# Cross-attention and routed FFN on one core: a transposition's copy on another engine, the router's scratch in another bank, and written-out orders for start and end

## What is computed

```python
def _L0_xattn_ref(input, encoded_features, Wq, bq, Wkv, bkv, Wo, bo):
    q = (input @ Wq + bq).reshape(b, tq, H, D).transpose(0, 2, 1, 3)
    kv = (encoded_features @ Wkv + bkv).reshape(b, tk, 2, H, D).transpose(2, 0, 3, 1, 4)
    scores = jnp.einsum('bhqd,bhkd->bhqk', q, k) / math.sqrt(D)
    attn = jax.nn.softmax(scores, axis=2)
    out = jnp.einsum('bhqk,bhkd->bhqd', attn, v)
    return out @ Wo + bo
def _L0_ffn_ref(x, w_router, w_block):
    scores = jnp.einsum('bld,d->bl', x, w_router)
    _, top_idx = jax.lax.top_k(scores, k)          # k = 96 of 128
    processed = jax.nn.gelu(jnp.einsum('bkd,de->bke', selected, w_block))
    return x.at[batch_idx, top_idx].set(processed)
x = x + _L0_xattn_ref(_layernorm(x), ctx, ...)
x = x + _L0_ffn_ref(_layernorm(x), w_router, w_block)
```

## Time and profile before

| what | value |
|---|---|
| runs | 956.96, 955.37, 956.26 us; median 956.26 |
| profiled execution, own time | 957.89 us |
| its span | 956.0 us |
| its mean granted TensorE clock | 0.985 |
| busy in the span | PE 892.5 (93%), ACT 894.6 (94%), DVE 849.6 (89%), POOL 814.4 (85%) |
| DMA | 70.84 MB, mean 74 GB/s |
| chain that ended last | PE 88%, ACT 5%, issue 2%, POOL 2% |

### The profile page before, as it was taken

The page is one execution under the profiler, slowest core; times in us unless marked ns, Lnnn a source line. Parts: engine busy times, 40 slices in busy tenths (PEclk is TensorE's granted clock), DMA queues, the critical chain, the costliest instruction groups (busy, mean ns, idle before and its releaser), DMA issues.

```text
span 956.0 us, 33133 instructions
## 1 busy us (share of the span) xinstructions
PE 892.5 (93%) x10276; PEld 757.0 (79%) x10276; DVE 849.6 (89%) x2568; ACT 894.6 (94%) x4612; POOL 814.4 (85%) x1514
## 2 busy tenths in 40 slices
PE   3699999999999999999999999999999999999870
PEld 2578888888888888888888888888888888888750
DVE  5688899999999999999999999999999999998754
ACT  2699999999999999999999999999999999999950
POOL 5257878999999999999999999999999999988777
PEclk9999999999999999999999999999999999999995
DMA  5222212322232232223223222322222232221102
GB/s 155 76 63 64 68 45 71 89 66 75 85 86 60 82 88 70 72 84 91 56 83 88 71 72 84 90 56 83 87 70 73 83 91 57 82 66 46 35 23 77
DMA packets 71245, 70.84 MB, mean 74 GB/s; under 512 B 12192, under 2 KB 62880, under 8 KB 71072
## 3 DMA queue, kind: packets, MB, share of 16 engines
q1 hardware_dynamic: 71072, 68.73, 25.2%
HBM read 35.13 MB, written 16.78 MB: 54 GB/s over the span
## 4 chain that ended last, share of the span: by engine, by line
PE 88%; ACT 5%; issue 2%; POOL 2%; DVE 1%; SPq 1%; DMA 1%; POOLq 0%; ACTq 0%; DVEq 0%
PE ps_q L272 18%; PE ps_s L306 14%; PE ps_a L355 13%; PE ps_a L279 12%; PE ps_t L279 11%; PE ps_a L272 9%; PE ps_t L327 8%; ACT e_sb L477 4%; PE ps_q L342 3%; DMA x_sb<-in_x 1%; POOL x_sb L834 1%; SPq L234 0%; POOL z_sb L817 0%; DVE neg_max L551 0%; PE ps_t L441 0%
## 5 line engine op out<-in xcount | busy, mean ns | idle before, releaser
L477 ACT ACTIVATE e_sb<-ps_s,neg_max 128x128 f32<-128x128 f32 x2048 | 724.9, 459 | 1.2 <-DVE neg_max L551 1.0
L477 ACT ACTIVATION_READ_ACCUMULATOR e_sb<-ps_s,neg_max 128x1 f32 x2048 | 588.3, 299 | 0.0
L551 DVE TENSOR_REDUCE neg_max<-ps_s 128x4 f32<-128x512 f32 x512 | 332.0, 669 | 64.4 <-PE ps_s L306 62.2
L306 PE MATMUL ps_s<-q_eo,k_sb 32*128 32x256 f32 x2048 | 146.8, 399 | 15.9 <-ACT e_sb L477 6.4
L768 POOL TENSOR_TENSOR v_pad<-v_sb,recip 128x256 f32<-128x256 f32 x128 | 79.6, 622 | 78.1 <-DVE recip L589 78.0
L355 PE MATMUL ps_a<-e_sb,v_pad 128*32 128x128 f32 x4096 | 138.4, 276 | 0.7 <-DVE x_sb L559 0.6
L279 PE MATMUL ps_a<-w_o_sb,o_sb 128*128 128x256 f32 x512 | 135.9, 388 | 2.9 <-DVE v_sb L635 2.4
L279 PE MATMUL ps_t<-w_z_sb,xt_sb 128*128 128x258 f32 x512 | 133.4, 383 | 2.9 <-DVE z_sb L646 2.9
L306 PEld LDWEIGHTS ps_s<-q_eo,k_sb 32*128 32x128 f32 x2048 | 95.8, 184 | 45.4 <-issue 42.4
L355 PEld LDWEIGHTS ps_a<-e_sb,v_pad 128*32 128x32 f32 x4096 | 104.1, 109 | 22.4 <-issue 21.2
L758 POOL TENSOR_TENSOR x_sb<-x_sb,bo_sb 128x256 f32<-128x256 f32 x128 | 121.3, 947 | 0.2
(11 more groups left out here) (80 smaller groups left out, 2249.2 us busy)
## 6 DMA issues: line engine op xcount, KB each, us to landing
x_sb<-in_x SPq DMA_DIRECT2D x64, 256.0 KB, 2.9
c_sb<-in_ctx SPq DMA_DIRECT2D x64, 256.0 KB, 3.1
q_eo<-q_raw SPq DMA_DIRECT2D x512, 32.0 KB, 2.0
out<-z_sb SPq DMA_DIRECT2D x64, 256.0 KB, 2.4
z_sb<-in_L_xattn_Wkv SPq DMA_DIRECT2D x2, 256.0 KB, 5.1
z_sb<-in_L_xattn_Wq SPq DMA_DIRECT2D x1, 256.0 KB, 2.9
w_o_sb<-in_L_xattn_Wo SPq DMA_DIRECT2D x1, 256.0 KB, 6.5
w_z_sb<-in_L_ffn_w_block SPq DMA_DIRECT2D x1, 256.0 KB, 5.5
```

The source lines that it names most:

```text
L306: mm = nc.tensor.matmul(ps_s[:, bank(b, j), c, :, :], k_sb[rows, r2, c, h * T:(h + 1) * T], q_eo[rows, r2, :, c, h, :], start=True, stop=True)
L477: last = nc.scalar.activation(e_sb[:, b % 4, j, c, par, :], ps_s[:, bank(b, j), c, par, :], ACT.Exp, bias=neg_max[:, b % 4, h:h + 1], accu ...
L551: nc.vector.tensor_reduce(neg_max[:, b % 4, :].rearrange("p (c j q) -> p j c q", c=C, j=J)[:, j, :, :], ps_s[:, bank(b, j), :, :, :], AX.X ...
```

## The change

It has five parts; names are those of the code.

1. `x1_transposed` (the copy of `ps_q`'s transposed x1 to xt_sb) goes from ACT to DVE, where it is the first work of each slot, ahead of the two aggregations and `maxima(s,3)`.
2. `fence` is gone: the aggregations and router steps carry their waits themselves.
3. The router's two transpositions write the fifth bank of `ps_s`. They wait for `exp_ready[0]` of an odd batch, `block_product` waits for the router no more, and in its place `scores(b)` waits for `cand_ready` when b mod 8 is 5 and for `keep_col_ready` when it is 1. The mean of the block weights goes through `ps_a`.
4. The first slots (up to the scores of batch 1) are written out for each engine. x of batches 2 and 3 is loaded fifth, not ninth; queries(0) stand behind the second transposition of inputs, not the third; batch 1's inputs are transposed into `ps_a`; the memset of q_eo is on POOL; the biases' semaphore is split; PE starts with 20 transpositions of the identity that nothing reads.
5. Behind the last scores each engine has an order of its own. `values(127)` goes ahead of `attention(126)`; the square in gelu of batches 123 to 127 is on ACT, the `(tanh+1)*z` of 121 to 127 is one instruction on DVE instead of two on POOL; `unprocessed` of 115 to 119 and 123 to 127 is on ACT; the router's last group runs in one piece.

The core of the diff (the order lists of the start and of DVE's and POOL's end are cut):

```diff
             return J if j == 0 and b % 2 == 1 else j
...
+        ps_cand, ps_keep, ps_mean = ps_fifth[0:GROUP, 0:T], ps_fifth[:, T:T + GROUP], ps_a[:, 0:ZW]
+        def inputs_bank(b):
+            return ps_a if b == 1 else ps_t
...
             load_c(0)
             sp.dma_start(raw_w["k"], w_kv[:, 0:E].rearrange("(c p) e -> p c e", p=P)).then_inc(w_in["k"], 16)
+            load_x(2)
...
-            load_x(2)
...
             pe.wait_ge(const_ready, 1)
+            for n in range(20):
+                nc.tensor.transpose(ps_s[:, 0, 0, n % 2, :], ident[:, :], ident[:, :])
...
                 if has(b - 2):
                     pe.wait_ge(exp_ready[0], upto(b - 2))
+                if b % GROUP == 5 and has(b - 13):
+                    pe.wait_ge(cand_ready, upto(b - 13 + 7))
+                if b % GROUP == 1 and has(b - 17):
+                    pe.wait_ge(keep_col_ready, upto(b - 17 + 7))
...
-                if b % GROUP == 0 and has(b - 8):
-                    pe.wait_ge(cand_ready, upto(b - 8 + 7))
-                if b % GROUP == 4 and has(b - 12):
-                    pe.wait_ge(keep_col_ready, upto(b - 12 + 7))
...
                     pe.wait_ge(z_ready, upto(b + 7))
-                    pe.wait_ge(t_lo_ready, upto(b + 17))
+                    pe.wait_ge(exp_ready[0], upto(b + 11))
...
-            for s in range(FIRST, LAST):
+            transpose_inputs(0)
+            transpose_inputs(1)
+            queries_or_keys(0, 0)
+            transpose_inputs(2)
+            queries_or_keys(0, 1)
+            transpose_inputs(3)
+            scores(0)
...
+            for s in range(2, B - 1):
...
+            scores(B - 1)
+            values(B - 2)
+            projection(B - 3)
+            block_product(B - 5)
+            transpose_x1(B - 4)
+            values(B - 1)
+            attention(B - 2)
+            keep_columns(B - 16)
+            transpose_x1(B - 3)
+            block_product(B - 4)
+            projection(B - 2)
+            attention(B - 1)
+            transpose_x1(B - 2)
+            projection(B - 1)
+            block_product(B - 3)
+            transpose_x1(B - 1)
+            block_product(B - 2)
+            block_product(B - 1)
+            candidates(B - 8)
+            keep_columns(B - 8)
...
-            def fence(n):
-
-                nc.vector.memset(fence_sb[:, n:n + 1], 0.0)
...
+            def x1_transposed(b):
+
+                if has(b):
+                    dve.wait_ge(xt_mm, upto(b))
+                    if has(b - 2):
+                        dve.wait_ge(z_mm, upto(b - 2))
+                    nc.vector.tensor_copy(xt_sb[:, b % 2, :], ps_xt).then_inc(xt_ready, 1)
...
+            def gelu_product(b):
+
+                dve.wait_ge(tanh_ready, upto(b))
+                nc.vector.scalar_tensor_tensor(z_sb[:, b % R, 0:E], g_sb[:, b % 4, :], 1.0, z_sb[:, b % R, 0:E],
+                                               ALU.add, ALU.mult).then_inc(gelu_dve_ready, 1)
...
+            for s in range(2, B):
+                x1_transposed(s - 4)
+                if s >= 4:
+                    stats1(s + 10)
                 aggregate2(s - 3)
                 router(s - 15, 6)
-                aggregate1(s + 10)
+                if s >= 4:
+                    aggregate1(s + 10)
                 maxima(s, 3)
```

More of the change, by code:

```diff
@@ L521, in _ @@
                 exps(s, 0)
+            attention_copy(B - 2)
+            gelu_square(B - 5)
+            gelu_tanh(B - 7)
+            gelu_square(B - 4)
+            attention_copy(B - 1)
+            gelu_tanh(B - 6)
+            for b in range(B - 13, B - 8):
+                unprocessed(b)
+            gelu_tanh(B - 5)
+            gelu_square(B - 3)
+            gelu_tanh(B - 4)
+            gelu_square(B - 2)
+            gelu_tanh(B - 3)
+            gelu_square(B - 1)
+            gelu_tanh(B - 2)
+            gelu_tanh(B - 1)
+            for b in range(B - 5, B):
+                unprocessed(b)
         @block.vector
@@ L718, in _ @@
                 router(s - 15, 9)
+                if s < 4:
+                    for b in range(2 * s + 6, 2 * s + 8):
+                        stats1(b)
+                        aggregate1(b)
+            x1_transposed(B - 4)
+            aggregate2(B - 3)
+            inverse_sums(B - 1)
+            router(B - 16, 10)
+            x1_transposed(B - 3)
+            product_scaled(B - 4)
+            gelu_product(B - 7)
+            residual(B - 2)
+            stats2(B - 2)
+            aggregate2(B - 2)
+            final(B - 16)
+            final(B - 15)
+            x1_transposed(B - 2)
+            gelu_product(B - 6)
+            residual(B - 1)
+            stats2(B - 1)
+            aggregate2(B - 1)
+            product_scaled(B - 3)
+            x1_transposed(B - 1)
+            final(B - 14)
+            gelu_product(B - 5)
+            product_scaled(B - 2)
+            final(B - 13)
+            final(B - 12)
+            gelu_product(B - 4)
+            product_scaled(B - 1)
+            final(B - 11)
+            for step in range(9):
+                router(B - 8, step)
+            router(B - 8, 9)
+            gelu_product(B - 3)
+            router(B - 8, 10)
+            gelu_product(B - 2)
+            gelu_product(B - 1)
+            final(B - 10)
+            final(B - 9)
+            for b in range(B - 8, B):
+                final(b)
         @block.gpsimd
@@ L849, in _ @@
                 gelu_product(s - 7)
+            rstd2_of_pair(B - 4)
+            gelu_factor(B - 5)
+            scale_and_shift(B - 16)
+            values_over_sums(B - 1)
+            gelu_cubic(B - 5)
+            unprocessed(B - 16)
+            unprocessed(B - 15)
+            rstd2_of_one(B - 2)
+            gelu_factor(B - 4)
+            gelu_cubic(B - 4)
+            unprocessed(B - 14)
+            rstd2_of_one(B - 1)
+            gelu_factor(B - 3)
+            gelu_cubic(B - 3)
+            gelu_factor(B - 2)
+            gelu_cubic(B - 2)
+            gelu_factor(B - 1)
+            gelu_cubic(B - 1)
+            scale_and_shift(B - 8)
+            for b in range(B - 8, B - 5):
+                unprocessed(b)
 _INS = ["x", "ctx_1024", "L0_xattn_Wq", "L0_xattn_bq", "L0_xattn_Wkv", "L0_xattn_bkv", "L0_xattn_Wo", "L0_xattn_bo",
```

260 lines of the change are left out of this document (189 added, 71 removed).

## The result

The changed kernel takes 938.7 us (median of 4 runs, 938.16 to 940.77), beside 956.1 for the kernel before (4 runs). The ratio is 0.9823, 95% interval 0.9811 to 0.9836: faster by 1.8%, where the prediction said 928.5 and at most 936.5.

The account below looks back on a forecast made before the run. Mid-program PE paces even halves and a PE-ACT-DVE loop odd ones; both ends have waits. From 957.9, slots -7.3, start -7.3, end -13.2 give 930.1, less 1.6 for the median: 928.5 us, range 922.5 to 936.5.

Parts of the forecast that it names:

- The slots: Repeated middle slots: copy off ACT and router's transpositions in the fifth bank save 0.50 per eight slots, -7.3 us in all.
- Rival A: Slots give nothing, since the copy delays maxima or v_sb where DVE's idle time is least: 935.8 us, 13%.
- The fences: DVE in each slot: their removal frees 0.18 us, so the copy of 0.41 adds only 0.23.
- The router's bank: PE's keep pair: the block product no longer waits for DVE's column read, 0.10 us per eight slots, bounds 0 and 0.18.
- The odd half: Odd-batch slots, a loop over three engines: down to 6.93 us once ACT loses the copy.
- The start: Before the slots: x(2) loads sooner, queries(0) at 10.3, first scores at 21.05, -7.3 us.
- rival C: Start: idle transpositions raise PE's clock, so queries(0) run faster: 927.5 us, 7%.
- The end: Last scores to last final's end: four stretches sum to 28.75 us against 41.96, -13.2.
- (b): End, attention(127) to the router's transposition: scaling z of 127 no longer stands behind finals, 11.28 to 7.65 us.
- (c): End, router to drop_rstd: no finals between its rounds, 9.94 to 4.1 us.
- (d): End, drop_rstd to the last final's end: twelve instructions close up at 0.43 each, 7.36 to 5.4 us.
- Rival F: End: DVE and POOL exclude each other in all twelve products and finals, +2.9 us, 931.4, 6%.

Follow-up runs that it names:

- run 1: Changed kernel with the copy of x1's transposition back on ACT inside the slots: 941.70 us.
- run 4: Kernel before with only the copy moved to DVE and no fences: 955.64 us beside 958.32, ratio 0.9969.
- run 5: Changed kernel with the inputs' statistics and aggregation moved behind the residual, one batch further ahead: 936.44 us beside 939.00.
- run 6: Changed kernel with one router step moved from the end of slot 5 to behind the inverse sums of slot 6: 936.75 us, ratio 0.9780.
- run 3: Changed kernel with the fence memsets put back ahead of both aggregations of every slot: 940.43 us.
- run 2: Changed kernel with the router's two transpositions back in the inputs' bank, with their old waits: 938.96 us.
- the control: Changed kernel run once more, unchanged, in the second group: 939.00 us.
- run 9: Changed kernel with 26 more identity transpositions on PE ahead of the first scores: 938.78 us beside 939.00.
- run 11: Kernel of run 9 with ACT's exponentials of batch 0, bank 1 ahead of t_hi of batch 5: 938.28 us, ratio 0.9795.
- run 8: Changed kernel with the finals of 115, 116 and 117 moved behind the router's last group: 938.17 us beside 939.00.
- run 10: Changed kernel without the 20 identity transpositions at PE's start: 939.40 us.

## Why the prediction was wrong

**The slots (-7.3 forecast, -3.1 measured).** The step that failed is "I price DVE's side at nothing, covered by 0.3 us; later work of the slot (v_sb, residual, q_raw) has DVE's idle time to catch up in". The cover was the wrong one. The maxima had 0.3 us of room; v_sb, behind them on the same engine, had about 0.1: it ended at 3.48 and is wanted, with 0.16 to pass on, by 3.56 for a projection at 3.72. And idle time was an average over eight slots, while the router's steps are not spread: slots 4, 5 and 7 have two, three and four of them. Behind those DVE starts the next slot late. Slot 6 pays 0.24 for that, in twelve slots from 22 to 110: 3.0 us. (Slots 14 and 118 did not grow: finals begin at slot 16, and slot 118 has no statistics left to take, so in both DVE has less to do.) Slot 5 starts its projection 0.1 late, but its odd half waits for exponentials anyway; slot 0 hides it behind the router's own transposition. Runs 1, 4, 5 and 6 show it. All in all the odd slots gave 6.1, which is the 6.0 forecast for them, and slot 6 took 3.0 back. Rival A had this mechanism, "where it is least, the copy delays maxima or v_sb", with 13%, and took the whole gain where 4.2 of 7.3 was lost; its sign, DVE busy 97% or more, came (195.36 of 200).

**The fences.** "The copy adds 0.41 - 0.18 = 0.23" counted the fences' busy time as time. Their rows lie inside those of other instructions, and run 3 shows no worth. The copy adds its 0.34 from one start to the next (397.54 to 397.88), and the maxima of slot 6 moved by 0.30.

**The router's bank.** "I take 0.10" was 0.00: run 2 and slot 0 at 7.12. The upper bound 0.18 held the transposition and a cost of PE beside it, no wait. That is 1.4 us.

**The odd half** was right: 6.91 to 6.94 where 6.93 was said.

**The start (-7.3, -6.3).** x(2) landed at 7.67 (7.8 said) and queries(0) began at 10.68 (10.3). The first scores came at 20.16 (21.05), since rival C held in this execution; that was luck of the clock, and in the control they came at 21.10. What failed is "the next two slots keep their length but for 0.1": 17.10 instead of 15.18. Two causes, by runs 9 and 11, one trace each: the lower clock after PE's idle 3.6 us (0.75 of it, and 0.15 more at scores(1)), and ACT's new order, in which t_hi of batch 5 stands ahead of exponentials that scores(1) need (0.72).

**The end (-13.2, -10.3).** Counted from the last scores:

| stretch | before | forecast | after |
|---|---|---|---|
| (a) to attention(127) | 13.38 | 11.6 | 11.53 |
| (b) to the candidates | 11.28 | 7.65 | 8.89 |
| (c) to drop_rstd | 9.94 | 4.1 | 4.66 |
| (d) to the last final's end | 7.36 | 5.4 | 6.04 |

What failed in (b) is "Finals now stand behind, and are fed by two engines: 11.28 - 2.2 - 1.4 = 7.65": two finals and a product still stood ahead of the scaling of z of 127, which began at 921.79, 0.9 after its matmuls. (b) was short by 1.24, of which run 8 gives back 0.87, 0.53 of it by who wins between DVE and POOL; the other 0.37 stays open. Rival F, that the two exclude each other, was priced at 2.9 for all twelve instructions and given 6%. It held for three instructions of (b) only: 0.94, 0.61 and 0.94 long where 0.48, 0.48 and 0.42 are undisturbed, 1.1 together. The ten finals of (d) took 0.47 to 0.49. (c): "four rounds of 0.35 (945.06 to 945.41) and about as much for the search, 0.69" left out a part: a round is 0.38 for the search, 0.08 for a load of the eight values and 0.37 for the replacement. The rounds start at 923.13 and 923.96, 0.83 apart:

```profile
923.13 0.28 DVE L773 MAX8 top<-cand 8x8 f32<-8x128 f32 x1
923.51 0.08 DVE L767 MATCH_VALUE_LOAD cand<-top,cand 8x8 f32 x1
923.59 0.26 DVE L767 MATCH_REPLACE8 cand<-top,cand 8x128 f32<-8x128 f32 x1
923.96 0.28 DVE L773 MAX8 top<-cand 8x8 f32<-8x128 f32 x1
```

(d): the finals of the three batches left on POOL still have 0.30 of wait each, and only the last ones close up at 0.40:

```profile
929.04 0.49 DVE L798 SCALAR_TENSOR_TENSOR z_sb<-z_sb,half_keep,x_sb 128x256 f32<-128x256 f32 x1 [0.30 <-POOL x_sb L1046]
...
930.61 2.46 DVE L798 SCALAR_TENSOR_TENSOR z_sb<-z_sb,half_keep,x_sb 128x256 f32<-128x256 f32 x6 [0.30 <-POOL x_sb L1046]
```

Behind the last final the stores take 3.1 to the end of the span, 0.5 more than before.

**The median.** The sum took 1.6 off for the runs' median; the after kernel's profiled execution stood 0.5 below its median instead, 2.1 in all. The range, 922.5 to 936.5, missed by 2.2. From 928.5 to 938.7 the slots make 4.2, the end 2.9, the start 1.0 and the executions' spread 2.1. The range treated errors of start, slots and end as independent; all had one direction, since each term took its gain and left out what the same change delays beside it.

## What to carry to other kernels

When work moves to an engine that waits, ask for the room of *each* result behind it on that engine, and in the fullest slot, not the mean one; the result with the least room sets the price, and it need not be the first in line. Before you take an instruction's busy time as its worth, look whether its row lies inside another's: the fences' did, and putting two of three back cost nothing that shows. A DVE instruction with two operands in SBUF beside a busy POOL can take twice its time (0.94 for 0.48), or POOL's can take half as much again (0.94 for 0.64), so weigh an operation moved between these two by what the other one does meanwhile.

## What the runs showed of the hardware that was not expected

- Transpositions of the identity can raise TensorE's clock: with 20 of them in front the inputs' first pair took 0.44 in eight of eleven traces and 0.69 in three, and 0.66 without (run 10). After 26 more the first scores took 1.15 in three of three, instead of 2.09 in eight of eight (run 9). The Trainium skill (TensorE: Matmul & The Clock Gate, "Part 4: PE-mode transpose") says that they don't count as busy the same way; these fp32 transpositions did raise it. Whether they ran in the mode that the section means, no row tells.
- DVE's final of two SBUF inputs and POOL's product, started 0.02 to 0.03 apart, took 0.94 and 0.64 in one kernel and 0.48 and 0.94 in another (run 8). No order there differs between the two; DVE lost where its row started 0.023 to 0.025 ahead of POOL's and won where it was 0.033 to 0.038 (ten traces). Who wins moved the end by 0.5. In the slots of run 5's kernel the finals, moved in time against POOL, took 0.59 in the middle of the order (median of those from 200 to 800 us), where they take 0.48 in the changed kernel.
